# A three-stage language-model tower: the front two units further ahead, and the layer norms' last step on Scalar

## The reference, cut to what matters

```python
h  = concat(emb_table[ids], upsampled STFT magnitudes of the one-hot ids @ proj_w + proj_b)   # 512 x 128
h  = h + attention(layernorm(h))        # 64 summary tokens, local window of 17, 8 heads
xn = layernorm(h)                       # (x - mean) / sqrt(var + 1e-5), no gain or bias
# top 2 of 8 experts; every expert's LSTM runs over the 16 sequences, on masked inputs
gates = xt @ Wi + hprev @ Wh + b ; c = sig(f)*c + sig(i)*tanh(g) ; hh = sig(o)*tanh(c)
y  = sum over chosen experts of weight * (hh @ Wo + bo)
out = h + y
```

## Time and profile before

| | |
|---|---|
| time, median of 3 runs | 1681.88 us |
| profiled execution | 1681.96 us, span 1680.2 us |
| TensorE (PE) busy | 1576.4 us, 94% |
| Vector (DVE) busy | 1524.8 us, 91% |
| Scalar (ACT) busy | 887.0 us, 53% |
| GpSimd (POOL) busy | 49.5 us, 3% |
| mean granted TensorE clock | 0.988 of full |

### The profile page before, as it was taken

The page is one execution under the profiler, slowest core; times in us unless marked ns, Lnnn a source line. Parts: engine busy times, 40 slices in busy tenths (PEclk is TensorE's granted clock), DMA queues, the critical chain, the costliest instruction groups (busy, mean ns, idle before and its releaser), DMA issues.

```text
span 1680.2 us, 21553 instructions
## 1 busy us (share of the span) xinstructions
PE 1576.4 (94%) x7416; PEld 757.3 (45%) x7416; DVE 1524.8 (91%) x2440; ACT 887.0 (53%) x1004; POOL 49.5 (3%) x43
## 2 busy tenths in 40 slices
PE   7767999999999999999999999999999999999998
PEld 3433444444444444444444444444444444444443
DVE  5578999999999999999999999999999999999876
ACT  4256545454554655545465554545546555454554
POOL 1000000000000000000000000000000000000000
PEclk8898999999999999999999999999999999999999
DMA  4133535344454454545446354454534445364452
GB/s 138 22 84 109 154 115 162 124 124 145 132 155 121 140 137 130 148 120 144 136 129 159 115 162 127 120 146 133 154 120 141 136 131 150 118 149 130 151 154 66
DMA packets 254766, 219.75 MB, mean 131 GB/s; under 512 B 131429, under 2 KB 174360, under 8 KB 254657
## 3 DMA queue, kind: packets, MB, share of 16 engines
q1 hardware_dynamic: 254576, 218.36, 45.5%
q10 hardware_dynamic: 80, 0.02, 0.0%
HBM read 73.06 MB, written 4.74 MB: 46 GB/s over the span
## 4 chain that ended last, share of the span: by engine, by line
PE 52%; DVE 36%; issue 8%; ACT 2%; DMA 1%; SPq 1%; POOL 0%; DVEq 0%; ACTq 0%
PE gates L584 14%; PE gates L583 14%; PE gates L578 11%; DVE C L1094 4%; DVE tmp L1118 4%; PE yp L590 3%; DVE H L1087 3%; DVE C L1122 3%; DVE H L1101 2%; DVE tmp L1111 2%; PE FA L523 2%; DVE z L1131 2%; PE FA L508 2%; ACT tmp L747 1%; DVE pr L966 1%
## 5 line engine op out<-in xcount | busy, mean ns | idle before, releaser
L747 ACT ACTIVATE tmp<-gates,bias_sb 128x1024 f32<-128x1024 f32 x504 | 558.5, 1111 | 505.2 <-PE gates L584 489.4
L584 PE MATMUL gates<-H,wh_sb 128*128 128x512 f32 x960 | 490.2, 592 | 0.0
L583 PE MATMUL gates<-H,wh_sb 128*128 128x512 f32 x960 | 490.2, 592 | 0.0
L578 PE MATMUL gates<-xm,wi_sb 128*128 128x512 f16 x1512 | 411.5, 381 | 6.4 <-ACT tmp L747 4.4
L584 PEld LDWEIGHTS gates<-H,wh_sb 128*128 128x128 f32 x960 | 182.4, 190 | 229.6 <-issue 229.6
L578 PEld LDWEIGHTS gates<-xm,wi_sb 128*128 128x128 f16 x1512 | 143.6, 99 | 282.6 <-issue 191.6
L754 ACT ACTIVATE tmp<-C 128x1024 f32<-128x1024 f32 x128 | 135.3, 1057 | 171.0 <-DVE C L1122 167.3
L583 PEld LDWEIGHTS gates<-H,wh_sb 128*128 128x128 f32 x960 | 182.3, 190 | 69.1
L1111 DVE SCALAR_TENSOR_TENSOR tmp<-tmp 128x1024 f32<-128x1024 f32 x120 | 145.2, 1210 | 36.2 <-ACT tmp L747 35.7
L1094 DVE COPY_PREDICATED C<-masks,Cx 128x1024 f32<-128x1024 uint16 x120 | 158.6, 1321 | 1.5 <-DMA Cx<-C 1.5
L1101 DVE SCALAR_TENSOR_TENSOR H<-tmp 128x1024 f32<-128x1024 f32 x128 | 155.9, 1218 | 2.1 <-ACT tmp L754 2.1
(11 more groups left out here) (167 smaller groups left out, 1246.2 us busy)
## 6 DMA issues: line engine op xcount, KB each, us to landing
Hx<-H SPq DMA_DIRECT2D x240, 256.0 KB, 2.6
Cx<-C SPq DMA_DIRECT2D x240, 256.0 KB, 2.4
masks<-mask_scratch SPq DMA_DIRECT2D x128, 256.0 KB, 5.1
roww<-mw_scratch SPq DMA_DIRECT2D x128, 256.0 KB, 3.4
diag<-pr SPq DMA_DIRECT2D x64, 112.0 KB, 3.1
diag<-vwin SPq DMA_DIRECT2D x64, 112.0 KB, 3.1
out_dram<-h SPq DMA_DIRECT2D x16, 256.0 KB, 2.7
C<-in_wi SPq DMA_DIRECT2D x1, 2048.0 KB, 10.8
```

What stands on the lines that cost most here:

```text
L578: mm(fed, wi_sb[:, e, wpart, rows_of], xm[:, e % 2, vpart, :], start=(wpart == HI and vpart == HI), stop=(first and wpart == LO))
L583: mm(fed, wh_sb[:, e, rows_of], H[:, e, 0:SEQ], start=False, stop=True)
L584: last = mm(other, wh_sb[:, e, rows_of], H[:, e, SEQ:2 * SEQ], start=True, stop=True)
L747: A(tmp[:, gate_at(gate, e), :], gates[:, (n - 1) % 2, :], ACT.Tanh, bias=bias_sb[:, e, gate:gate + 1], scale=UNSCALE).then_inc(s_tanh, 1)
```

## The change

- All pieces of the front stand one to two slots earlier (a few by another amount), and EARLY is 10.
- The embedding's product goes into the first half of FA instead of FB. It waits for `attn` of the sequence before; the wait for the mask and weight rows' copies moves from it to the transposes `xT`.
- Both norms are applied by ACT: out = rstd * x + shift, with rstd and shift one value per token, in four operations of 128 columns. DVE makes shift = -mean * rstd (one operation on 4 columns) where it applied the norm before.
- DVE's `add_y` at t = 7 stands ahead of the swap of C instead of behind.

```diff
--- before.py
+++ after.py
@@ -53,15 +53,15 @@
     Q_SCALE = 2.0 ** 4
 
 
-    SP_AT = dict(ids=-8, qbd=1, vz=5, rows=25, wrow=28)
-    PE_AT = dict(emb=-5, xT=-2, qkv=-1, summary=2, window=4, feature=10, values=15, proj=17, projT=18, x2T=20,
+    SP_AT = dict(ids=-10, qbd=-1, vz=3, rows=25, wrow=28)
+    PE_AT = dict(emb=-7, xT=-4, qkv=-3, summary=0, window=2, feature=8, values=13, proj=16, projT=17, x2T=20,
                  logits=21, maskT=25)
-    ACT_AT = dict(h=-5, xT=-2, qkv=-1, split=0, summary=4, window=7, pr_hi=11, feature=12, proj=17, x2T=20,
+    ACT_AT = dict(h=-7, xn=-5, xn2=18, xT=-4, qkv=-3, split=-2, summary=2, window=5, pr_hi=9, feature=10, proj=16, x2T=20,
                   choice=22, maskT=25)
-    DVE_AT = dict(onehot=-6, moments=-4, xn=-3, pw=0, q_lo=0, kv_lo=1, v_win=2, w_max=3, s_max=5, s_sub=6, w_sum=7,
-                  w_out=8, s_sum=9, s_norm=10, f_max=11, p_lo=12, p_T=13, f_sum=14, f_part=14, attn=15,
-                  moments2=18, xn2=19, x_lo=21, choice1=22, choice2=22, weights=23)
-    EARLY = 8
+    DVE_AT = dict(onehot=-8, moments=-6, xn=-5, pw=-2, q_lo=-2, kv_lo=-1, v_win=0, w_max=1, s_max=3, s_sub=4, w_sum=5,
+                  w_out=6, s_sum=7, s_norm=8, f_max=9, p_lo=10, p_T=11, f_sum=12, f_part=12, attn=14,
+                  moments2=17, xn2=18, x_lo=21, choice1=22, choice2=22, weights=23)
+    EARLY = 10
     MASKS_AT = 26
     YT_AT, YBACK_AT, YADD_AT = 5, 6, 7
     WT0 = 64
@@ -104,6 +104,7 @@
         veps = sb("veps", [P, TILES])
         spare = sb("spare", [P, 1])
         rstd = sb("rstd", [P, TILES])
+        shift = sb("shift", [P, TILES])
         xn = sb("xn", [P, TILES, D])
         xnT = sb("xnT", [P, SEQ])
         qT = sb("qT", [P, SEQ])
@@ -255,7 +256,7 @@
         s_yadd = sem("s_yadd")
         s_out = sem("s_out")
 
-        names = """ids enc onehot emb hsb bnst bnag veps rstd xn xnTp xnT qp kp vp q k v qbd vwin vz
+        names = """ids enc onehot emb hsb bnst bnag veps rstd shift shift2 xn xnTp xnT qp kp vp q k v qbd vwin vz
             pw sw mw dw ew rw iw ow owr ow_c pf sf mf df ef rf if_ uf S mS dS eS rS iS prT O of0
             khi vhi qhi qlo klo vlo pn phi plo cf attn projT projS proj h2 bnst2 bnag2 veps2 rstd2 xn2 x2p xhi x32 xlo lgp lg m1 eq1 ix1 im1 k1 l2 m2
             eq2 ix2 im2 k2 dd ed sd w0 w1 wa wb sel ne sw_ mwc mwp mrow wT mout wout ybo"""
@@ -490,15 +491,17 @@
                     pe.wait_ge(S["onehot"], b1)
                     pe.wait_ge(S["enc"], 16 * b1)
                     if not is_zero(b):
-                        pe.wait_ge(S["mrow"], b)
-                        pe.wait_ge(S["wT"], b)
+                        pe.wait_ge(S["attn"], b)
                     for i in range(TILES):
-                        last = mm(FB[:, i * D:(i + 1) * D], rows[0:ENC0 + NFR, i * P:(i + 1) * P], table[:, :],
+                        last = mm(FA[:, 0, i * D:(i + 1) * D], rows[0:ENC0 + NFR, i * P:(i + 1) * P], table[:, :],
                                   start=True, stop=True)
                     last.then_inc(S["emb"], 1)
                 if t == PE_AT["xT"]:
                     pe.wait_ge(S["xn"], b1)
                     pe.wait_ge(S["hsb"], b1)
+                    if not is_zero(b):
+                        pe.wait_ge(S["mrow"], b)
+                        pe.wait_ge(S["wT"], b)
                     for i in range(TILES):
                         last = nc.tensor.transpose(FB[:, i * P:(i + 1) * P], xn[:, i, :], ident[:, :])
                     last.then_inc(S["xnTp"], 1)
@@ -671,7 +674,18 @@
                     act.wait_ge(S["emb"], b1)
                     if not is_zero(b):
                         act.wait_ge(S["h2"], b)
-                    A(h_sb[:, :, :].rearrange("p t d -> p (t d)"), FB[:, :], ACT.Copy).then_inc(S["hsb"], 1)
+                    A(h_sb[:, :, :].rearrange("p t d -> p (t d)"), FA[:, 0, :], ACT.Copy).then_inc(S["hsb"], 1)
+                if t == ACT_AT["xn"]:
+                    act.wait_ge(S["shift"], b1)
+                    for i in range(TILES):
+                        last = A(xn[:, i, :], h_sb[:, i, :], ACT.Identity, bias=shift[:, i:i + 1], scale=rstd[:, i:i + 1])
+                    last.then_inc(S["xn"], 1)
+                if t == ACT_AT["xn2"]:
+                    act.wait_ge(S["shift2"], b1)
+                    for i in range(TILES):
+                        last = A(xn[:, i, :], h2[:, par_of(b), i, :], ACT.Identity, bias=shift[:, i:i + 1],
+                                 scale=rstd[:, i:i + 1])
+                    last.then_inc(S["xn2"], 1)
                 if t == ACT_AT["xT"]:
                     act.wait_ge(S["xnTp"], b1)
                     A(xnT[:, :], FB[:, :], ACT.Copy).then_inc(S["xnT"], 1)
@@ -878,13 +892,11 @@
                     last.then_inc(S["bnag"], 1)
                     wait("bnag", b1)
                     TS(veps[:, :], mv[:, :, 1], EPS, None, ALU.add).then_inc(S["veps"], 1)
-                for at, ready, src, dst in (("xn", "rstd", lambda i: h_sb[:, i, :], "xn"),
-                                            ("xn2", "rstd2", lambda i: h2[:, q, i, :], "xn2")):
+                for at, ready, done in (("xn", "rstd", "shift"), ("xn2", "rstd2", "shift2")):
                     if t == DVE_AT[at]:
                         wait(ready, b1)
-                        for i in range(TILES):
-                            last = TS(xn[:, i, :], src(i), mv[:, i, 0:1], rstd[:, i:i + 1], ALU.subtract, ALU.mult)
-                        last.then_inc(S[dst], 1)
+                        STT(out=shift[:, :], in0=mv[:, :, 0], scalar=-1.0, in1=rstd[:, :],
+                            op0=ALU.mult, op1=ALU.mult).then_inc(S[done], 1)
                 if t == DVE_AT["pw"]:
                     wait("q", b1)
                     wait("k", b1)
@@ -1151,6 +1163,8 @@
                     if t == XM_AT and not last:
                         masked_input(s + 1, 0, 1 - par, False)
                         swap_h(s + 1, 0)
+                    if t == YADD_AT and not first:
+                        add_y(s - 1, 1 - par)
                     if g == 3 and e < E - 1 and not first:
                         swap_c(s, e + 1)
                     elif g == 3 and e == E - 1 and not last:
@@ -1159,8 +1173,6 @@
                         chosen(s, e - 1)
                     elif g == 2 and not first:
                         chosen(s - 1, E - 1)
-                    if t == YADD_AT and not first:
-                        add_y(s - 1, 1 - par)
                     run_front(lambda u, b: front(u, b, b % 2), t, s)
                     if g == 1:
                         input_part(s, e, first)
```

## The result

The changed kernel took 1689.39 us, the median of six runs (1685.89 to 1691.38), against 1681.53 of six of the kernel before beside it: a ratio of 1.0048, 95% interval 1.0038 to 1.0059. It is 0.5% slower, where 0.35% faster was forecast. The profiled execution took 1690.87 us.

The account below looks back on a forecast made before the run. With TensorE and Vector both nearly full, the longest dependence ring was taken as the bound: 100.8 + 0.3 + 0.15 + 0.25 = 101.5 us a period. 1681.96 - 6.2 - 1.5 + 2 = 1676.3, say 1676 us; range 1663 to 1690.

Parts of the forecast that it names:

- The ring: Slot 29: Vector's shift, xn on Scalar, transposes, unit 29, its tanh, Vector's product and queue; 100.8 us a period.
- the way back: From Vector's shift through Scalar and TensorE to Vector's input product at slot 29: 5.8 us.
- Scalar's group: One norm as four 128-column operations on Scalar: 1.45 to 1.5 us, bounds 1.1 and 2.0.
- The three small waits: Waits (a), (b) and (c) lying on the ring: 0.3, 0.15 and 0.25 us a period.
- (a): Second norm: Vector's work does not quite cover GpSimd's power; 0.3 us stays open (0 to 0.4).
- (b): Scalar waits at slot 18 for the shift, delaying tanhs that Vector's slot 20 product needs: 0.15 us (0 to 0.65).
- (c): Slots 29 to 3: TensorE's stretch and two tanhs end later than Vector's stretch by 0.25 us (0 to 0.6).
- The ring, not the waits, sets the period: TensorE's waits only move, still about 3.4 to 4 us a step; the add_y wait grows to 1.3 us.
- The ends: Outside the thirteen periods: last step -1.5 us, prologue together +2 us.
- Rival 3: Slower through Scalar's queue at slot 18, Vector waiting 0.65 at slot 20: 102.5 a period, 1689 to 1690 us, chance 0.24.
- Rival 1: The ring closes without (a) to (c), or Scalar's group takes 1.1 us: 100.8 a period, 1666 us, chance 0.22.
- Rivals 2 and 4: 2: TensorE was the bound, 1632 us, chance 0.05; 4: the ring never closes, within 2 us of 1681, 0.04.

Follow-up runs that it names:

- The first experiment: The changed kernel with the first norm alone back on Vector, the second staying on Scalar: 1675.53 us, ratio 0.9966.
- the two repairs: The changed kernel with y_bias and expert 0's y product behind unit 9, 1675.26 us; or with four filler products ahead of the add_y wait, 1678.04 us.
- the best version: The changed kernel with first-norm transposes to score subtraction one slot later, and the onehot one slot earlier: 1637.4 us, ratio 0.9742.
- the opened schedule: The changed kernel with first-norm transposes (behind unit 29) to score subtraction one slot later: 1644.26 us; with both norms on Vector 1660.51 us.

## Why the prediction was wrong

- **The ring.** Right. It closed at slot 29 through Scalar, TensorE's transposes, unit 29 and its tanh, with a wait of 4.8 us on Vector. The first experiment shortens it by its Scalar part, and the transposes behind unit 29 take 3.07 us off the period, 1.96 of it beyond what the clock gives. Vector's work (96.26 for 96.15) and the way back (5.94 for 5.8) came as sized.
- **Scalar's group.** The rows were read for 1.5 us, the records show 1.65: four operations of 477 to 495 ns. The upper half of the bounds held it. The rule that was set against the rows was the better one: the Trainium skill, ScalarE: Activation LUTs, What ACT_TABLE_LOAD costs, gives an estimated 0.48 us for one with two pointer operands and 1.64 for the group, and this trace agrees. No run here has one pointer operand on 128 columns, so the price of the second alone isn't shown. The 0.14 a period it adds is small beside the miss.
- **The three small waits.** (a) 0.30, as forecast. (b), at slot 20, is absent for 0.15. (c), at slot 4, is 0.06 for 0.25.
- **The step that failed: "The ring, not the waits, sets the period", with the wait for add_y at nothing.** The growth of the add_y wait was foreseen (1.3, measured 1.22), and held harmless because TensorE wasn't the bound. It stands between units 8 and 9, and on this ring Vector has spare time only at slot 29: any unit late by more than TensorE's lead lengthens the period. The wait of 1.22 us alone is within that lead: the two periods that have it at full clock are 101.47 and 101.49, where 101.5 was forecast. What the forecast put at nothing, without a reason, is the clock behind the wait: it fell to 0.50 in eleven of the thirteen periods, and unit 9 came 1.5 us later still. That is 1.11 us a period, shown by keeping TensorE busy ahead of the wait, which leaves the order as it was, and in line with taking unit 9 out from behind the wait, which changes both. With it gone the period is 101.23 to 101.24 and the time 1675 to 1678, where 1676 was forecast. That these times meet the forecast one is partly luck: their periods are shorter than forecast and their starts later.
- **The ends.** The last step gained 2.7 us, 1.5 was forecast. The start lost 4.8 instead of 2. The cause stays open. The change's shift puts mask transposes and embedding on one slot of the prologue, whose filler table has room for one entry a slot, and 11 fillers are lost. The first `y_bias` ran at half the clock: 1056 to 1217 ns a record, 587 to 692 before (the first rows of the two source views above), and with more fillers still. But the fillers' 2.2 us lies within the 3.8 by which two executions of one program differed, and so does what the run with the split moved says of the 1.3 for xn behind the weight split. The forecast's pw, q_lo and kv_lo ahead of the first masked input (2.3) are there too in the run with both norms on Vector, which started at 105.9, so the runs don't bear that term out either.
- **The rivals.** Rival 3 gave the right time, 1689 to 1690, by another mechanism: Vector's wait at slot 20 for Scalar's queue, its place, did not come. Rival 1's ring without waits is what the two repairs nearly reach (101.24, of which 0.30 is wait (a), against 100.8). Rivals 2 and 4 did not occur, though TensorE does become the bound in the best version.

## What to carry to other kernels

Where two full engines hand work back and forth, follow the ring that a moved step closes, and put the consumer behind the unit whose result the producer waits for, not ahead of it: here one slot was worth 1.96 us of 102, and 3.07 with the clock. A wait that grows on TensorE where it "isn't the bound" is to be costed with the clock that may fall behind it, and it is cheap to test by filling it with work. Whether an operation belongs on the slower but idler engine depends on whether it is on the ring: at full clock the same eight operations on Scalar were worth nothing that can be told while the ring was closed, and 0.80 us a period once it was open. And before two mean periods are compared, look at each step's clock: of the 1.87 us between two of these kernels 1.07 was the clock.

## What the runs showed of the hardware that was not expected

- A short stand of TensorE can be followed by some 3 us at 0.50 of the clock, and the same stand need not be. The 1.22 us wait for add_y was followed by it in six of eight periods, the 1.11 us wait for the onehot in five of eight with both norms on Vector in the opened schedule, and the 2.6 us wait for the second norm's xn, with the norms on Scalar without the shift, in five of eight. The 1.89 us wait for xn in the kernel before and the 1.09 us wait at the first norm's transposes (below, the changed kernel) were followed by none. What parts them is open:

```profile
564.00:566.00 2.00, 0.93 (x3) 0.10 (x1) 1.42 (x3) 1.78 (x6) 0.00 (x0) 1.00 0.14 24
566.00:568.00 2.00, 1.98 (x9) 1.25 (x10) 0.00 (x0) 1.45 (x2) 0.00 (x0) 1.00 0.82 101
568.00:570.00 2.00, 2.00 (x6) 0.95 (x5) 0.00 (x0) 0.93 (x1) 0.00 (x0) 1.00 0.97 328
```

- GpSimd's power on 128x4 took 1.91 to 1.95 us in all 18 instances between 400 and 1300 us, where it was 1.01 where Vector stood waiting for it. Vector now has work beside both norms. Source view:

```profile
L1216 POOL TENSOR_TENSOR rstd<-veps,mhalf x18: 1912/1924/1949, 432.2 to 1276.6; 128x4 f32<-128x4 f32 x18
```
